# Second attention hop: the row mean taken directly behind the residual sums, with 40 filler matmuls instead of 48; mean layer: a tile's rows and turned rows in one transfer

## The chip, the cores and the metric

The kernel runs on one core of a Trainium2 chip. The metric is the time of one execution on the device, in microseconds (us), the median of three runs. A profile is one further execution, recorded by the hardware profiler. Engines are PE (TensorE), DVE (VectorE), ACT (ScalarE), POOL (GpSimd) and SP (SyncE), which issues most of the transfers here. "SPq", "DVEq" and so on are the sequencers of these engines: they load registers, compute with them, wait for semaphores, and hand work to the engine.

## What is computed

Four graph layers run over 50000 nodes of 256 values and 25000 edges, each followed by a residual sum and a layer norm. The two that the change touches are the first layer and the second hop of the third:

```python
# layer 0 (the kernel's mean layer)
agg = segment_sum(edge_weight[:, None] * x[dst], src)
out = concatenate([agg, x], axis=1) @ W.T
out = (out - mu) * rsqrt(var + 1e-5) * gamma + beta
x = layernorm(x + relu(out))
...
# layer 2 (attention), two hops
e = leaky(sum(([x[head], x[tail]] @ fc_w.T + fc_b) * rel_e, axis=-1))
w = exp(e - max of the head's edges) / their sum
x = sum over the head's edges of w * x[tail], plus x
x = x / max(norm(x), 1e-12)
...
x = layernorm(x_before_layer_2 + x)
```

## The kernel before

The kernel is a row of phases with a barrier between them: sorting the edges, the mean layer (`l0`), a message phase and relation layer twice, two attention hops (`l2a`, `l2b`), and the last layer. Rows lie in 391 tiles of 128 nodes. An *item* is a tile together with up to 128 of its edges. Every engine runs its own program over the items. There is no scheduler: the order on each engine is the hand-written tuple of steps, each with a number that says how many pairs (or octets) it runs ahead of the loop's count, and semaphores tie the engines together.

**Mean layer** (`mean_layer`, from L772). Items are done in pairs, a ring of 8 slots (`RING`), with a loop body of 4 pairs. `load_groups` gives the number of loop turns, items divided by 8 and rounded up. Per item PE sums the gathered edge rows into `ps_a` (L879) and multiplies the tile's turned rows (L889) and the sums (L892) by the weights; ACT takes `ps_b` and does squares and the last scaling (L767); DVE does the rest. SP (`move_tiles`, L145 on) issues per item three transfers of 128 KB: the rows `x` and the turned rows `x_t` into their slots (L160), and the result (L186). At the head of each loop turn it reads three lists of 8 row numbers into registers (L153). POOL (`gather_rows`) issues two indirect gathers per pair of items (L215), and between them (`between`) scatters for a later phase (L289), 200 of `item_records` and 20 of `rel_source_rows`, six for every five pairs. It waits for PE's sums of the pair four earlier before it reuses a slot.

**Second hop** (`attention_hop` with `last_hop`). Items are done in octets of 8, the loop body has two octets, and `load_hops` gives the number of turns, items divided by 16 and rounded up. In one octet's turn of the loop, with the lines that the prediction uses:

- DVE: `add_residual` of octet 0 (L1976, 8 sums over rows that also leave the row sum), `find_slots` (L1716, its sequencer reads 8 slot numbers into registers), `scores` (L1898 to L1905), `divide` (L1924 to L1929), `add_up` in two halves (L1914), with `centre` (L732, minus the row mean) between the halves, `add_self` (L1940), `maximum` (L1945 to L1957), `have_square` (L1964), `find_nodes` (L1885 on), and small steps of an inverse root up to L1631.
- ACT: `norm.square` of the octet (L741), which needs the mean; `measure` (L2018), `decay` (L2027, needs `minus` from L1957), guesses (L1614, L1616), `chances` (L2035), two copies to `hot` (L2043), and the last scaling (L767).
- PE: sums of 8 items (L2079), `spread` (L2089, L2091), 48 fillers (L700), `turn_chances` first half (L2098), 4 fillers, second half, `look_up` (L2111), 4 fillers. A filler is a matmul of zeros whose result nobody reads; `keep_busy` writes them.

A `pass_wait` is a wait of the sequencer by itself, followed by an increment; a plain `wait_ge` goes into the instruction behind it.

Of the kernel before, what the change touches and what calls it, by code (L numbers as in the profile page):

```python
# [30 lines left out]
P = 128  # L31
# [164 lines left out]
            sp.sem_inc(s["passed"], 1)  # L196


def gather_rows(pool, graph, s, index, gathered, source, extra=0, field=OTHER, count=N_NODES, between=None):
# [12 lines left out]
    fixed = TILES // RING  # L212

    def gather_by(slot, rows):
        pool.indirect_dma_start(gathered[:, slot, 0:D], None, source[0:count, :], bass.IndirectOffsetOnAxis(ap=rows, axis=0),  # L215
                                bounds_check=limit, oob_is_err=False).then_inc(s["in_g"][slot // 2], 16)

    def gather(pair, slot):
        both = slice(slot, slot + 2)
        pool.tensor_copy(index[:, both, 0], graph.meta[:, bass.ds(pair * 2, 2), field].bitcast(I32))\  # L220
            .then_inc(s["index_copied"], 1)
        pool.wait_ge(s["index_copied"], pair + 1)
        pool.sem_inc(s["passed"], 1)
        for k in (slot, slot + 1):
            gather_by(k, index[:, k, :])

    groups = load_groups(pool, graph)
    for pair in range(fixed * PAIRS):
        if pair >= PAIRS:
            pool.wait_ge(s[s["g_last"]], pair * 2 + 2 - RING)  # L230
        for item in (2 * pair, 2 * pair + 1):
            gather_by(item % RING, graph.meta[:, item, field:field + 1].bitcast(I32))
        if between is not None:
            between(pair)
    pool.sem_inc(s["index_copied"], fixed * PAIRS)
    with pool.Fori(fixed - 1, groups) as g:
        for n in range(PAIRS):
            pair = g * PAIRS + n
            pool.wait_ge(s[s["g_last"]], pair * 2 + 2)
            pool.sem_inc(s["passed"], 1)  # L240
            gather(pair + PAIRS, 2 * n)
    for n in range(extra // 2):
        pool.wait_ge(s[s["g_last"]], groups * RING + 2 * n + 2)
        pool.sem_inc(s["passed"], 1)
        gather((groups + 1) * PAIRS + n, 2 * n)
    for n in range(PAIRS):
        pool.wait_ge(s["in_g"][n], (groups + 1 + (2 * n < extra)) * 32)
        pool.sem_inc(s["passed"], 1)
# [445 lines left out]
        eng.wait_ge(sem, self.item + 2)  # L694


def keep_busy(pe, c, spare, n):

    for _ in range(n):
        pe.matmul(spare, c.ones_b[:], c.zero_row[:], start=True, stop=True)  # L700


def run_pairs(eng, graph, steps):


    groups = load_groups(eng, graph)
    for n in range(-max(ahead for _, ahead in steps), 0):
        for step, ahead in steps:
            if n + ahead >= 0:
                step(Pair(0, n + ahead))  # L710
    with eng.Fori(0, groups) as g:
        for n in range(PAIRS):
            for step, ahead in steps:
                step(Pair(g, n + ahead))


class Norm:
# [51 lines left out]
                .then_inc(s["out_ready"] if done is None else done, 1)  # L769


def mean_layer(nc, c, graph, w, gamma, beta, eps, x_in, x_in_t, x_out, relations, edges, records, rel_source):  # L772

    with Phase(nc, "l0") as ph:
        x, gathered, agg_t, x_t, products, scaled, shifted, summed, result = (
            ph.sb(k, [P, RING, D], F32) for k in ("x", "gathered", "agg_t", "x_t", "products", "scaled", "shifted",
                                                  "summed", "result"))
# [7 lines left out]
        s["in_xt"] = [ph.sem(f"in_xt{k}") for k in range(RING)]  # L785
        s_records, s_sources = ([ph.pool_dma_sem(f"{n}{k}") for k in range(2)] for n in ("records", "sources"))
        inner, outer = Norm(ph, "inner", eps), Norm(ph, "outer", eps)
        with nc.Block() as block:
            @block.sync
            def _(sp):  # L790
                later = ((x_t, x_in_t, s["in_xt"], s["b_done"], 6),)
                move_tiles(sp, graph, s, x, x_in, result, x_out, later, lead=2)

            @block.gpsimd
            def _(pool):
                by_dst = Scatter(pool, s_records, records[:], edges.place, lambda column: edges.records[:, column, :])
                sources = Scatter(pool, s_sources, rel_source[:], relations.place,
                                  lambda column: relations.source[:, column:column + 1])
# [8 lines left out]
                gather_rows(pool, graph, s, index, gathered, x_in, extra=2, between=between)  # L807
                by_dst.finish()
                sources.finish()
                assert by_dst.sent == EC and sources.sent == EC - SOURCES_BEFORE  # L810

            @block.vector
            def _(dve):
# [18 lines left out]
                def combine(pair):  # L832
# [8 lines left out]
                    for j, k in pair.each():  # L841
                        pass_wait(dve, s, s["in_x"][k], (pair.lap + 1) * 16)
                        dve.wait_ge(s["shifted"], j + 1)
                        dve.scalar_tensor_tensor(summed[:, k, :], shifted[:, k, :], 0.0, x[:, k, :], ALU.max, ALU.add,
                                                 accum_out=outer.sum[:, k:k + 1]).then_inc(s["summed"], 1)

                def centre_outer(pair):
# [7 lines left out]
                make(Pair(0, 0))  # L855
                run_pairs(dve, graph, ((lambda p: inner.invert(dve, p), 1), (centre_inner, 2), (combine, 1),
                                       (lambda p: outer.invert(dve, p), 0), (lambda p: outer.shift(dve, p), 0),
                                       (accumulate, 5), (centre_outer, 1)))

# [1 line left out]
            def _(act):  # L861
                def take(pair):
                    for j, k in pair.each():
# [4 lines left out]
                run_pairs(act, graph, ((lambda p: outer.spread(act, p, summed), 0),  # L868
                                       (lambda p: inner.spread(act, p, products), 2), (take, 3),
                                       (lambda p: outer.apply(act, s, p, result, summed), 0)))  # L870

# [1 line left out]
            def _(pe):  # L873
# [7 lines left out]
                        last.then_inc(s["a_done"], 1)  # L881

                def product(pair):
                    for j, k in pair.each():
                        if not isinstance(j, int) or j >= 4:
                            pe.wait_ge(s["products"], j - 3)
                        pe.wait_ge(s["in_xt"][k], (pair.lap + 1) * 16)
                        for i in range(2):
                            pe.matmul(ps_b[k % 4], x_t[:, k, i * P:(i + 1) * P], w[:, 2 + i, :], start=(i == 0), stop=False)  # L889
# [796 lines left out]
def attention_hop(nc, c, graph, name, node_rows, w, x_in, x_out, residual=None):  # L1686
# [6 lines left out]
    with Phase(nc, name) as ph:  # L1693
# [46 lines left out]
        with nc.Block() as block:  # L1740
# [133 lines left out]
            def _(dve):  # L1874
# [195 lines left out]
            def _(pe):  # L2070
# [172 lines left out]
def build(nc, a, out):  # L2243
# [3 lines left out]
    with ExitStack() as ctx:  # L2247
# [13 lines left out]
        with ExitStack() as first:  # L2261
# [7 lines left out]
            with ExitStack() as prep:  # L2269
                def sb_prep(name, shape, dt):  # L2270
                    return prep.enter_context(nc.sbuf_tensor(name, shape, dt))
                for g, n in zip(graphs, ("src", "dst")):
# [5 lines left out]
            mean_layer(nc, c, by_src, w.l0, w.gamma, w.beta, w.eps, a["x"], a["x_turned"], x1, relations, edges,  # L2278
                       item_records[1], rel_source)
            count_edges_and_message(nc, c, graphs, node_rows, relations, item_records[1], rel_source, "ma", a["L1_gnn_W1"], x1,  # L2280
                                    messages)
# [9 lines left out]
def laid_out(inputs):  # L2291
# [2 lines left out]
    x = np.zeros((ALL_ROWS, D), np.float32)  # L2294
    x[:N_NODES] = a["x"]
    a["x"] = x
    a["x_turned"] = x.reshape(-1, P, 2, P).transpose(0, 3, 2, 1).reshape(ALL_ROWS, D)
# [22 lines left out]
```

## Time and profile before

| | us |
|---|---|
| median of 3 runs | 6965.96 (6964.8 to 6974.53) |
| profiled execution | 6984.61 |
| its span, first to last instruction | 6982.7 |
| mean granted clock of PE over the span | 0.933 |

Of the span, PE is busy 90%, DVE 76%, ACT 61%, POOL 56%. The mean layer lies at 702 to 1677 us and the second hop at 4926 to 5914 us. A clock of 1.00 is 2.4 GHz, 0.50 is 1.2 GHz. Matmuls are pipelined: the duration that is shown for one reaches past the start of the next, so what one costs is read from start to start.

### The profile page before, as it was taken

What the parts mean: (1) busy time and instruction counts of PE and PEld (TensorE: products, weight loads), DVE (VectorE), ACT (ScalarE), POOL (GpSimd) and SP (SyncE); (2) the same over time, 40 slices, a digit from 0 to 9 for tenths busy, and PEclk for the clock granted to TensorE, in tenths of its full rate; (3) what the DMA queues carried; (4) which work ended last, traced back from release to release, by engine and by line L of the source; (5) the groups of instructions that cost most, each with busy time, mean ns of one, the idle gap of its engine ahead of it and who ended that gap; (6) DMA issues with size and microseconds to landing.
All of it is one profiled execution on the core that took longest, in us unless ns stands there. A gap on an engine that the chain in (4) does not pass through costs nothing. (4 is left out here: it accounts for less than half of the span.)

```text
span 6982.7 us, 169103 instructions
## 1 busy us (share of the span) xinstructions
PE 6298.9 (90%) x37102; PEld 5098.3 (73%) x37103; DVE 5285.4 (76%) x18168; ACT 4280.0 (61%) x14748; POOL 3904.1 (56%) x3592
## 2 busy tenths in 40 slices
PE   5676899997789998989999899999899998999999
PEld 2222788886688887769999788888566666888887
DVE  9887888887655654247777677777688887899998
ACT  0000899995214443238888677777588787677777
POOL 6677777775736666754444444444444444444443
PEclk9555999998879999999999899999899999999999
DMA  1200666666656666667777666665577676444443
GB/s 40 6 2 8 182 193 193 194 194 192 182 154 192 199 197 186 198 186 222 222 222 222 178 185 187 186 187 173 176 221 216 205 221 184 123 126 127 128 127 118
DMA packets 1224976, 1161.36 MB, mean 166 GB/s; under 512 B 314483, under 2 KB 1152523, under 8 KB 1224094
## 3 DMA queue, kind: packets, MB, share of 16 engines
q1 hardware_dynamic: 1067230, 943.02, 43.9%
q0 software_dynamic: 157632, 217.06, 13.3%
q8 instruction: 42, 0.69, 0.0%
q14 instruction: 72, 0.59, 0.0%
HBM read 946.93 MB, written 395.69 MB: 192 GB/s over the span
## 5 line engine op out<-in xcount | busy, mean ns | idle before, releaser
L215 POOL DMA_INDIRECT l_gathered<-x,by_dst_meta x384 | 433.6, 1129 | 547.7 <-PE l_ps_a L1571 485.8
L1836 POOL DMA_INDIRECT l2b_gathered<-z,by_src_meta x408 | 431.1, 1057 | 534.9 <-PE l2b_ps_g L2079 419.6
L1836 POOL DMA_INDIRECT l2a_gathered<-x,by_src_meta x408 | 431.1, 1057 | 453.8 <-PE l2a_ps_g L2079 338.1
L215 POOL DMA_INDIRECT l1b_gathered<-messages,by_dst_meta x384 | 395.3, 1029 | 437.8 <-PE l1b_ps_b L1434 376.8
L215 POOL DMA_INDIRECT l1a_gathered<-messages,by_dst_meta x384 | 432.1, 1125 | 206.7 <-PE l1a_ps_b L1434 141.7
L700 PE MATMUL l2b_ps_x<-zero_row,ones_b 128*128 128x392 bf16 x2912 | 510.1, 330 | 0.0
L215 POOL DMA_INDIRECT l_gathered<-in_x,by_src_meta x384 | 417.7, 1088 | 130.7 <-issue 113.9
L889 PE MATMUL l_ps_b<-l_w,l_x_t 128*128 128x256 f32 x1592 | 416.2, 384 | 38.8 <-DMA l_x_t<-in_x_turned 37.8
L865 ACT ACT_TABLE_LOAD x1 | 1.3, 1283 | 702.6 <-PEq L129 702.6
L1432 PE MATMUL l1b_ps_b<-root,l1b_x_t 128*128 128x256 f32 x1600 | 425.8, 389 | 0.0
L1432 PE MATMUL l1a_ps_b<-root,l1a_x_t 128*128 128x256 f32 x1584 | 415.6, 385 | 3.8 <-DVE l1a_hot L670 1.6
L700 PEld LDWEIGHTS l2b_ps_x<-zero_row,ones_b 128*128 128x128 bf16 x2912 | 286.1, 100 | 178.8 <-issue 0.9
L1388 ACT ACTIVATE l1a_x_t<-l1a_ps_x,by_dst_first 128x256 f32<-128x256 f32 x400 | 167.6, 470 | 401.4 <-PE l1a_ps_x L1420 401.4
L892 PE MATMUL l_ps_b<-l_w,l_agg_t 128*128 128x256 f32 x1592 | 409.0, 379 | 0.0
L1590 PE MATMUL l_ps_b<-l_w,l_mix_t 128*128 128x256 f32 x1592 | 396.5, 392 | 8.9 <-DVE l_mix_t L1506 8.8
L1338 DVE SCALAR_TENSOR_TENSOR l1a_total<-l1a_total,by_dst_keep,l1a_ps_b 128x256 f32<-128x256 f32 x394 | 187.1, 475 | 270.3 <-PE l1a_ps_b L1434 270.3
L1586 PE MATMUL l_ps_b<-l_w,l_x_t 128*128 128x256 f32 x1592 | 384.3, 384 | 1.0 <-ACT l_x_t L1551 1.0
L633 PE MATMUL sort_ps_rank<-sort_onehot,not_before 125*125 125x392 bf16 x400 | 234.6, 587 | 162.6 <-DVE sort_junk L583 162.6
L1590 PEld LDWEIGHTS l_ps_b<-l_w,l_mix_t 128*128 128x128 f32 x1592 | 286.3, 189 | 114.7 <-DVE l_mix_t L1506 83.6
L633 PEld LDWEIGHTS sort_ps_rank<-sort_onehot,not_before 125*125 125x125 bf16 x400 | 72.0, 180 | 384.8 <-DVE sort_junk L583 384.8
L889 PEld LDWEIGHTS l_ps_b<-l_w,l_x_t 128*128 128x128 f32 x1592 | 284.5, 191 | 86.7 <-DMA l_x_t<-in_x_turned 31.2
L892 PEld LDWEIGHTS l_ps_b<-l_w,l_agg_t 128*128 128x128 f32 x1592 | 303.0, 190 | 41.4
(402 smaller groups left out, 20682.5 us busy)
## 6 DMA issues: line engine op xcount, KB each, us to landing
x<-l1b_result SPq DMA_DIRECT2D x400, 152.0 KB, 3.0
z<-l2a_result SPq DMA_DIRECT2D x400, 152.0 KB
l2a_x<-x SPq DMA_DIRECT2D x53, 1024.0 KB
l2b_x<-z SPq DMA_DIRECT2D x53, 1024.0 KB
l1b_x<-h SPq DMA_DIRECT2D x408, 128.0 KB
l1b_res<-x SPq DMA_DIRECT2D x408, 128.0 KB
l2b_res<-x SPq DMA_DIRECT2D x51, 1024.0 KB
l_x_t<-in_x_turned SPq DMA_DIRECT2D x406, 128.0 KB
```

Of the source, the lines that this page charges most:

```text
L215: pool.indirect_dma_start(gathered[:, slot, 0:D], None, source[0:count, :], bass.IndirectOffsetOnAxis(ap=rows, axis=0), bounds_check=limit ...
L633: pe.matmul(rank[o][0:EP, :], c.not_before[0:EP, 0:EP], onehot[0:EP, o, k, :], start=False, stop=True, skip_group_check=True)
L700: pe.matmul(spare, c.ones_b[:], c.zero_row[:], start=True, stop=True)
L865: act.activation(products[:, k, :], ps_b[k % 4], ACT.Identity, accum_out=inner.sum[:, k:k + 1])\
L889: pe.matmul(ps_b[k % 4], x_t[:, k, i * P:(i + 1) * P], w[:, 2 + i, :], start=(i == 0), stop=False)
L892: last = pe.matmul(ps_b[k % 4], agg_t[:, k, i * P:(i + 1) * P], w[:, i, :], start=False, stop=(i == 1))
L1338: dve.scalar_tensor_tensor(total[:, k, :], total[:, (k - 1) % RING, :], graph.keep[:, bass.ds(j, 1)], ps_b[k // 2 % 2][:, k % 2, :], ALU.m ...
L1388: act.activation(x_t[:, k, :], ps_x[k // 2 % 2][:, k % 2, :], ACT.Copy, scale=graph.first[:, bass.ds(j, 1)]).then_inc(s["xt"], 1)
L1432: pe.matmul(sums, x_t[:, k, f * P:(f + 1) * P], root[:, f, :], start=(f == 0), stop=False)
L1586: pe.matmul(ps_b[k % 4], x_t[:, k, i * P:(i + 1) * P], w1[:, i, :], start=(i == 0), stop=False)
L1590: last = pe.matmul(ps_b[k % 4], mix_t[:, k, i * P:(i + 1) * P], w2[:, i, :], start=False, stop=(i == 1))
L1836: pool.indirect_dma_start(gathered[:, k, :], None, x_in[0:N_NODES, :], bass.IndirectOffsetOnAxis(ap=rows, axis=0), bounds_check=limit, oob ...
```

## The change

Three edits. In the second hop, `centre` moves on DVE from between the halves of `add_up` to directly behind `add_residual`, ahead of `find_slots`. The row of 48 fillers there becomes 40. In the mean layer, the host lays rows and turned rows side by side (`x_both`, 512 values a row), and one transfer of 256 KB brings both, into a ring of 16 slots; the loop body has 8 pairs, so the number of items is rounded up to a multiple of 16 and no longer of 8. The gathers still read `x`.

```diff
+        both = ph.sb("both", [P, HOP, 2 * D], F32)
+        x, x_t = both[:, :, 0:D], both[:, :, D:2 * D]
...
-                later = ((x_t, x_in_t, s["in_xt"], s["b_done"], 6),)
-                move_tiles(sp, graph, s, x, x_in, result, x_out, later, lead=2)
...
+                def load(row, slot):
+                    sp.dma_start(both[:, slot, :], x_both[bass.ds(row, P), :]).then_inc(in_both[slot], 16)
+
+                for half in range(2):
+                    rows = rows_of(load_regs, LOAD, half * RING)
+                    for k in range(RING):
+                        load(rows[k], half * RING + k)
...
+                hops = load_hops(sp, graph)
+                with sp.Fori(0, hops) as g:
+                    for half in range(2):
+                        first = g * HOP + half * RING
+                        rows = rows_of(store_regs, STORE, first)
+                        next_rows = rows_of(load_regs, LOAD, first + HOP)
+                        for k in range(RING):
+                            sp.wait_ge(s["summed"], first + (k + 1))
+                            load(next_rows[k], half * RING + k)
+                            sp.wait_ge(s["out_ready"], first + (k + 1))
+                            sp.dma_start(x_out[bass.ds(rows[k], P), :], result[:, k, :]).then_inc(s["stored"][k], 16)
...
-    groups = load_groups(pool, graph)
+    groups = load_hops(pool, graph) * 2 if wide else load_groups(pool, graph)
...
-                run_pairs(pe, graph, ((product, 3), (gather_sum, 5)))
+                run_wide_pairs(pe, graph, ((product, 3), (gather_sum, 5)))
...
-                    steps = [(add_residual, 0), (find_slots, 1), (scores, 2), (divide, 1), (part(add_up, 0), 1), (centre, 0), (part(add_up, 1), 1),
+                    steps = [(add_residual, 0), (centre, 0), (find_slots, 1), (scores, 2), (divide, 1), (part(add_up, 0), 1), (part(add_up, 1), 1),
...
-                        (spread, 2), (part(fill, 48), 2), (part(turn_chances, 0), 2), (part(fill, 4), 2),
+                        (spread, 2), (part(fill, 40), 2), (part(turn_chances, 0), 2), (part(fill, 4), 2),
```

The move on DVE, second hop, in the loop body's second octet. Before, from the last residual sum to behind the mean:

```order
L1976 SCALAR_TENSOR_TENSOR l2b_y,l2b_norm_sum<-l2b_y,l2b_inv_root,l2b_res 128x256
L1716 ISA
L1716 TENSOR_LOAD by_src_table
L1657 REGISTER_ALU
L1898 TENSOR_TENSOR l2b_both<-l2b_ps_s,l2b_gathered 128x192
...
L1914 SCALAR_TENSOR_TENSOR l2b_agg<-l2b_agg,l2b_shrink,l2b_ps_g 128x256 x2
L732 TENSOR_SCALAR l2b_norm_minus_mean<-l2b_norm_sum 128x8
```

and of the changed kernel, in the same place:

```order
L2035 SCALAR_TENSOR_TENSOR l2b_y,l2b_norm_sum<-l2b_y,l2b_inv_root,l2b_res 128x256
L758 TENSOR_SCALAR l2b_norm_minus_mean<-l2b_norm_sum 128x8
L1775 ISA
L1775 TENSOR_LOAD by_src_table
L1716 REGISTER_ALU
L1957 TENSOR_TENSOR l2b_both<-l2b_ps_s,l2b_gathered 128x192
```

The mean, which waits for the last residual sum, now stands ahead of the sequencer's read of the slot numbers (TENSOR_LOAD), and with it ahead of `scores`. Line numbers grow by 26 or 59.

On SP, mean layer, the head of the loop body up to the third transfer. Before:

```order
L153 TENSOR_LOAD by_src_table
L154 ISA
L153 ISA
L153 TENSOR_LOAD by_src_table
L154 ISA
L153 ISA
L153 TENSOR_LOAD by_src_table
L154 ISA
L160 DMA l_x<-in_x 128x256
L160 DMA l_x_t<-in_x_turned 128x256
L186 DMA x<-l_result 128x256
```

and of the changed kernel:

```order
L821 TENSOR_LOAD by_src_table
L822 ISA
L821 ISA
L821 TENSOR_LOAD by_src_table
L822 ISA
L825 DMA l_both<-in_x_both 128x512
L845 DMA x<-l_result 128x256
```

Eight items cost SP three lists and 24 transfers before, and two lists and 16 transfers now.

## Rows read from the trace of the kernel before

**Rows 1.** Stretches: busy us of PE, PEld, DVE, ACT, POOL; clock, DMA share, GB/s
```profile
900.00:1200.00 300.00, 284.67 (x1524) 247.53 (x1523) 262.43 (x1080) 274.79 (x1016) 237.65 (x205) 1.00 0.68 193
5100.00:5400.00 300.00, 289.03 (x1801) 207.40 (x1799) 262.01 (x911) 252.25 (x990) 130.86 (x126) 1.00 0.73 218
```
**Rows 2.** Timeline of SP, mean layer: start us, us, engine, line, operation, names
```profile
1250.12 0.36 SPq L186 DMA_DIRECT2D x<-l_result  x1
1255.97 0.34 SPq L160 DMA_DIRECT2D l_x<-in_x  x1
...
1268.99 0.36 SPq L186 DMA_DIRECT2D x<-l_result  x1
```
**Rows 3.** What POOL waited for, 900 to 1200 us: total, times, longest
```profile
POOL l_gathered L215 <- issue: 38.5, 126, 0.3
POOL item_records L289 <- issue: 23.6, 77, 0.3
```
**Rows 4.** Timeline of POOL, mean layer: its first gather, and one of the last
```profile
705.63 1.05 POOL L215 DMA_INDIRECT l_gathered<-in_x,by_src_meta  x1 [1.65 <-issue]
...
1567.38 1.02 POOL L215 DMA_INDIRECT l_gathered<-in_x,by_src_meta  x1 [0.30 <-issue]
```
**Rows 5.** Timeline of PE, mean layer: first sums, and two pairs at the end
```profile
710.19 2.08 PE L879 MATMUL l_ps_a<-l_hot,l_gathered 128*128 128x128 f32 x8 [11.49 <-DMA l_gathered<-in_x,by_src_meta]
...
1653.27 1.05 PE L879 MATMUL l_ps_a<-l_hot,l_gathered 128*128 128x128 f32 x8
...
1657.62 1.05 PE L879 MATMUL l_ps_a<-l_hot,l_gathered 128*128 128x128 f32 x8
```
**Rows 6.** Timeline of SP: mean layer's last store, next phase's first transfer
```profile
1669.92 0.36 SPq L186 DMA_DIRECT2D x<-l_result  x1
1676.98 0.33 SPq L949 DMA_DIRECT2D rel_index<-rel_source_rows  x1
```
**Rows 7.** Timeline of DVE, second hop: loop body's first octet, sums and scores
```profile
5219.28 0.49 DVE L1976 SCALAR_TENSOR_TENSOR l2b_y<-l2b_y,l2b_inv_root,l2b_res 128x256 f32<-128x256 f32 x1 [1.04 <-DMA l2b_res<-x]
...
5222.54 0.35 DVE L1898 TENSOR_TENSOR l2b_both<-l2b_ps_s,l2b_gathered 128x192 f32<-128x192 f32 x1
...
5223.71 0.17 DVE L1905 SCALAR_TENSOR_TENSOR l2b_score<-l2b_plain 128x8 f32<-128x8 f32 x1
```
**Rows 8.** Timeline of DVE, second octet of the same loop body
```profile
5237.62 0.49 DVE L1976 SCALAR_TENSOR_TENSOR l2b_y<-l2b_y,l2b_inv_root,l2b_res 128x256 f32<-128x256 f32 x1 [0.42 <-DVE l2b_inv_root L1631]
...
5241.23 0.36 DVE L1898 TENSOR_TENSOR l2b_both<-l2b_ps_s,l2b_gathered 128x192 f32<-128x192 f32 x1 [0.27 <-PE l2b_ps_s L2111]
```
**Rows 9.** DVE's sequencer at L1716 and L664, 5219.5 to 5224.5
```profile
L1716 DVEq TENSOR_LOAD <-by_src_table x1: 594/594/594, 5220.6 to 5220.6; - x1
...
L664 DVEq ALU_OP  x2: 40/40/40, 5223.7 to 5223.9; - x2
```
**Rows 10.** Timeline of PE, second hop: fillers, and `turn_chances` in both octets
```profile
5190.35 8.12 PE L700 MATMUL l2b_ps_x<-zero_row,ones_b 128*128 128x392 bf16 x48
5199.25 0.66 PE L2098 MATMUL l2b_ps_e<-ident,l2b_chance 128*128 128x128 f32 x4 [0.77 <-ACT l2b_chance L2035]
...
5217.83 0.66 PE L2098 MATMUL l2b_ps_e<-ident,l2b_chance 128*128 128x128 f32 x4 [0.28 <-ACT l2b_chance L2035]
```
**Rows 11.** Timeline of PE: the two longest of these waits, and the third
```profile
5123.58 0.66 PE L2098 MATMUL l2b_ps_e<-ident,l2b_chance 128*128 128x128 f32 x4 [1.29 <-ACT l2b_chance L2035]
...
5428.41 0.66 PE L2098 MATMUL l2b_ps_e<-ident,l2b_chance 128*128 128x128 f32 x4 [1.98 <-ACT l2b_chance L2035]
...
5546.95 0.66 PE L2098 MATMUL l2b_ps_e<-ident,l2b_chance 128*128 128x128 f32 x4 [1.74 <-ACT l2b_chance L2035]
```
**Rows 12.** Stretch behind the second, PE: busy us (x), clock, DMA share, GB/s
```profile
5429.00:5439.00 10.00, 10.00 (x38) 0.51 0.41 109
```
**Rows 13.** Timeline of DVE: first sum of this octet, and of the next
```profile
5428.94 0.48 DVE L1976 SCALAR_TENSOR_TENSOR l2b_y<-l2b_y,l2b_inv_root,l2b_res 128x256 f32<-128x256 f32 x1 [0.42 <-DVE l2b_inv_root L1631]
...
5452.43 0.48 DVE L1976 SCALAR_TENSOR_TENSOR l2b_y<-l2b_y,l2b_inv_root,l2b_res 128x256 f32<-128x256 f32 x1 [1.04 <-issue]
```

More of the change, by code:

```diff
@@ L196, in move_tiles, with gather_rows @@
             sp.sem_inc(s["passed"], 1)
-def gather_rows(pool, graph, s, index, gathered, source, extra=0, field=OTHER, count=N_NODES, between=None):
+def gather_rows(pool, graph, s, index, gathered, source, extra=0, field=OTHER, count=N_NODES, between=None, wide=False):
     limit = pool.alloc_register(f"limit_{s['name']}")
@@ L694, in wait_items, with __init__, each_wide @@
         eng.wait_ge(sem, self.item + 2)
+class WidePair(Pair):
+    def __init__(self, group, n):
+        super().__init__(group * 2, n)
+        self.wide = 2 * n % HOP
+        self.wide_lap = group + n // RING
+    def each_wide(self):
+        return [(self.item + q, self.slot + q, self.wide + q) for q in range(2)]
 def keep_busy(pe, c, spare, n):
@@ L714, in run_pairs, with run_wide_pairs @@
                 step(Pair(g, n + ahead))
+def run_wide_pairs(eng, graph, steps):
+    hops = load_hops(eng, graph)
+    for n in range(-max(ahead for _, ahead in steps), 0):
+        for step, ahead in steps:
+            if n + ahead >= 0:
+                step(WidePair(0, n + ahead))
+    with eng.Fori(0, hops) as g:
+        for n in range(RING):
+            for step, ahead in steps:
+                step(WidePair(g, n + ahead))
 class Norm:
@@ L769, in apply, with mean_layer @@
                 .then_inc(s["out_ready"] if done is None else done, 1)
[L772 removed]
+def mean_layer(nc, c, graph, w, gamma, beta, eps, x_in, x_both, x_out, relations, edges, records, rel_source):
     with Phase(nc, "l0") as ph:
[L775 to L777 removed]
+        gathered, agg_t, products, scaled, shifted, summed, result = (
+            ph.sb(k, [P, RING, D], F32) for k in ("gathered", "agg_t", "products", "scaled", "shifted", "summed", "result"))
+        both = ph.sb("both", [P, HOP, 2 * D], F32)
+        x, x_t = both[:, :, 0:D], both[:, :, D:2 * D]
         index = ph.sb("index", [P, RING, 1], I32)
@@ L784, in mean_layer @@
             s[k] = ph.sem(k)
-        s["in_xt"] = [ph.sem(f"in_xt{k}") for k in range(RING)]
+        in_both = s["in_x"] + [ph.sem(f"in_x{k}") for k in range(RING, HOP)]
         s_records, s_sources = ([ph.pool_dma_sem(f"{n}{k}") for k in range(2)] for n in ("records", "sources"))
@@ L790, in _, with rows_of @@
             def _(sp):
-                later = ((x_t, x_in_t, s["in_xt"], s["b_done"], 6),)
-                move_tiles(sp, graph, s, x, x_in, result, x_out, later, lead=2)
+                store_regs, load_regs = ([sp.alloc_register(f"l0_{n}_{k}") for k in range(RING)] for n in ("store", "load"))
+                def rows_of(regs, field, first_item):
+                    sp.load(regs, graph.table[0:1, field, bass.ds(first_item, RING)])
+                    return [sp.snap(r, min_val=0, max_val=ALL_ROWS - P) for r in regs]
+                def load(row, slot):
[4 more added lines that the diff above has]
+                        load(rows[k], half * RING + k)
+                sp.wait_ge(s["zeroed"], 2)
+                for slot in range(RING):
+                    sp.dma_start(x_out[ROWS + slot * P:ROWS + (slot + 1) * P, :], result[:, slot, :])\
+                        .then_inc(s["stored"][slot], 16)
+                hops = load_hops(sp, graph)
[9 more added lines that the diff above has]
+                            sp.dma_start(x_out[bass.ds(rows[k], P), :], result[:, k, :]).then_inc(s["stored"][k], 16)
+                for slot in range(RING):
+                    sp.wait_ge(s["stored"][slot], (hops * 2 + 1) * 16)
+                    sp.sem_inc(s["passed"], 1)
+                for slot in range(HOP):
+                    sp.wait_ge(in_both[slot], (hops + 1) * 16)
+                    sp.sem_inc(s["passed"], 1)
             @block.gpsimd
@@ L805, in between @@
                             sources.send(SOURCES_BEFORE + n - EC)
-                gather_rows(pool, graph, s, index, gathered, x_in, extra=2, between=between)
+                gather_rows(pool, graph, s, index, gathered, x_in, extra=2, between=between, wide=True)
                 by_dst.finish()
@@ L840, in combine @@
                                                  ALU.mult, ALU.add).then_inc(s["shifted"], 1)
-                    for j, k in pair.each():
-                        pass_wait(dve, s, s["in_x"][k], (pair.lap + 1) * 16)
+                    for j, k, m in pair.each_wide():
+                        pass_wait(dve, s, in_both[m], (pair.wide_lap + 1) * 16)
                         dve.wait_ge(s["shifted"], j + 1)
-                        dve.scalar_tensor_tensor(summed[:, k, :], shifted[:, k, :], 0.0, x[:, k, :], ALU.max, ALU.add,
+                        dve.scalar_tensor_tensor(summed[:, k, :], shifted[:, k, :], 0.0, x[:, m, :], ALU.max, ALU.add,
                                                  accum_out=outer.sum[:, k:k + 1]).then_inc(s["summed"], 1)
@@ L854, in _ @@
                 dve.sem_inc(s["acc"], 1)
-                make(Pair(0, 0))
-                run_pairs(dve, graph, ((lambda p: inner.invert(dve, p), 1), (centre_inner, 2), (combine, 1),
+                make(WidePair(0, 0))
+                run_wide_pairs(dve, graph, ((lambda p: inner.invert(dve, p), 1), (centre_inner, 2), (combine, 1),
                                        (lambda p: outer.invert(dve, p), 0), (lambda p: outer.shift(dve, p), 0),
@@ L883, in product @@
                 def product(pair):
-                    for j, k in pair.each():
+                    for j, k, m in pair.each_wide():
                         if not isinstance(j, int) or j >= 4:
                             pe.wait_ge(s["products"], j - 3)
-                        pe.wait_ge(s["in_xt"][k], (pair.lap + 1) * 16)
+                        pe.wait_ge(in_both[m], (pair.wide_lap + 1) * 16)
                         for i in range(2):
-                            pe.matmul(ps_b[k % 4], x_t[:, k, i * P:(i + 1) * P], w[:, 2 + i, :], start=(i == 0), stop=False)
+                            pe.matmul(ps_b[k % 4], x_t[:, m, i * P:(i + 1) * P], w[:, 2 + i, :], start=(i == 0), stop=False)
                         pe.wait_ge(s["acc"], j + 2)
```

6 lines of the change are left out of this document (3 added, 3 removed).

## The prediction

> **What bounds the kernel now.** First the stretches of both places. In the mean layer POOL's busy time [rows 1] and its gaps, none above 0.3 us [rows 3], make 237.65 + 38.5 + 23.6 = 299.75 of 300 us: POOL is at its pace. SP is too. From the last store of one loop turn to that of the next is 18.87 us for 8 items, and between that store and the next transfer lie 5.85 us [rows 2], in which it reads three lists of row numbers. So (18.87 - 5.85) / 23 = 0.57 us is one transfer's pace. Both engines do 8 items in about 19 us: POOL's 183 pairs from 705.63 to 1567.38 [rows 4] are 4.71 us each, 18.8 us per 8 items. PE could go faster: at the end, with its gathers ahead of it, two pairs lie 1657.62 - 1653.27 = 4.35 us apart [rows 5].
>
> In the second hop PE is busy 289 of 300 us [rows 1], but the loop is not PE's: much of that are fillers, 48 in a row with 8.12 / 49 = 0.166 us from one to the next, the last being shown twice as long [rows 10]. Behind them PE waits 0.77 us in the turn that ends the first octet and 0.28 us in the other, for ACT's `chances`. DVE waits almost nowhere: its first sum follows its own inverse root (0.42 us) or the 1.04 us of the loop's head [rows 7, 8]. The loop goes by DVE's steps, and by the ring DVE, `decay` on ACT, `chances`, PE. From the wait at 5123.58 to that at 5428.41 lie 16 octets [rows 11]: 304.83 / 16 = 19.05 us each, 38.1 us a turn. The first octet's 5237.62 - 5219.28 = 18.34 us [rows 7, 8] leave 19.8 us for the second, with the loop's head. 25 turns make the hop.
>
> **Mean layer, part by part.** *Transfers.* 8 items now cost SP 16 transfers and two lists instead of 24 and three: 16 x 0.57 + 5.85 x 2/3 = 13.0 us. That is below POOL's 18.8, so SP stops being a bound. POOL's work is unchanged, and it stays the next one, so the middle of the layer gains nothing. What ends is SP's lag at the tail. *Two halves of 8 pairs.* The count is rounded up to 16 items: 392 becomes 400, which is 4 pairs more. POOL's gather at 1567.38 is that of pair 184 of 200 [rows 4], and all scatters are issued by then. Its sums can follow by 710.19 - 705.63 = 4.6 us [rows 4, 5], at 1572. From there on PE is the bound with 20 more pair steps at 4.35 us: 1572 + 87 = 1659. I put the last store about 3 us behind, at 1662, and the next phase's first transfer 1676.98 - 1669.92 = 7.06 us behind that [rows 6], at 1669: **-8 us**. From below, if SP's lag was also what held the pairs before (11 us of PE's lag behind POOL at the end), -13. From above, if POOL's gathers or the rows' larger transfers make PE later by three pairs' time, +6.
>
> **Second hop: the mean.** The edit moves one 128x8 instruction, which itself costs 0.11 us where it stood and 0.12 where it goes. What matters is what it stands ahead of. DVE's sequencer reads the slot numbers in 0.594 us at 5220.6, in the midst of the eight sums, which it has handed over by then: the read is hidden, and `scores` start at 5222.54, 3.26 us behind the first sum [rows 7, 9]. The sums wait for nothing that runs on DVE just then. The mean waits for the last of them. What a waiting instruction does to the sequencer the trace shows at L1905, which waits for the step before it: it starts at 5223.71, and the two register steps of L664 that stand behind it start at 5223.7 and 5223.9 [rows 7, 9], although nothing else held them. So the sequencer stood until L1905 went, and I take it that it will stand at the mean too. Then the order is mean at +3.36, 0.12 for it to go, 0.60 for the read, 0.40 for some ten register steps of 40 ns each, `scores` at **+4.48**. Net in the first octet 4.48 - 3.26 = 1.22, less the 0.11 saved later: 1.11 us. In the second octet `scores` start at 3.61 [rows 8], of which 0.27 is a wait for PE that is covered now; the median over the octets is 3.51, so 4.48 - 3.51 - 0.11 = 0.86. Together 2.0 us a turn, 25 turns: 50 us. Waits for the residual rows ahead of the first sum, some 4 us over the hop, vanish in it: **+46 us**. From below: if the read is still hidden, the term is 2 x -0.11 x 25 = -5. From above, if the read takes its place among busy transfers and is slower by half, +60. I take 46, since L1905 and L664 are the same sequencer in the same loop.
>
> The Trainium skill says otherwise. By "Perfetto Trace Analysis", section "DVE / Act Engine Instruction", a DVE instruction is pushed into a wait queue, and the sequencer decodes the next one before its semaphores are satisfied. By that rule the read stays hidden and the sum loses its 46 us; rows 9 show L664 behind L1905's start, which speaks against it.
>
> **Second hop: 40 fillers.** They aren't on the ring's path, so the 8 that go save nothing by themselves; PE waits 8 x 0.166 = 1.33 us longer. To that comes what `chances` are later by: the waits become 0.77 + 1.11 + 1.33 = 3.2 us and 0.28 + 0.86 + 1.33 = 2.5 us. Nobody needs PE earlier; what the fillers keep up is its clock. Of the waits at this place, 1.29 us left the clock at 1.00, and the two longest, 1.74 and 1.98 us [rows 11], were followed by a clock of 0.51, which is the lower of the two levels, 1.2 GHz [rows 12]. The octet in which it ran low, a second one of its turn, took 5452.43 - 5428.94 = 23.49 us from first sum to first sum [rows 13], where its place takes 19.8, or 19.6 without the waits for residual rows that are in the 46 already: 3.9 us more. The other one took 22.61 (5547.50 to 5570.11), 3.0 more. Both new waits are longer than those that were followed by a fall. But while the matmuls run low, PE is late and has no wait at all, so the next wait comes an octet later: I count one fall per turn. It costs (3.9 + 3.0) / 2 = 3.5, less the 0.9 us by which `scores` now come later in any case, so that a late PE holds them less: 2.6 us. 25 x 2.6 = 65, less the 7 us of the two falls that are in the time already: **+58 us**. From below, none: -7. From above, each at 3.9: 98 - 7 = 91.
>
> **Sum.** -8 + 46 + 58 = +96 us. The profiled execution took 6984.61 us, 6982.7 of it the span; with the sum it is 7080.6. It lies 18.65 us above the median of the runs, which I carry over: **7062 us**. Its own range, with the ends above where they go together: 7025 to 7100.
>
> **Rivals.**
> *The read is exposed, but the clock mostly stays.* For it: only two waits above 1.7 us are there to judge by, and the one of 1.29 us left no mark on the clock [rows 11]. Against it: both were followed by a fall. -8 + 46 - 7 = +31: 6997 us.
> *The read stays hidden, and the clock falls.* The scores come where they did, and the waits are 0.77 - 0.11 + 1.33 = 2.0 and 1.5 us: the first is as long as those that fell. Half of 25 turns at 3.5 is 44, less 7; with -8 and -5: +24, 6990 us. If every turn falls, 7033.
> *Nothing is exposed (the other side).* The read stays hidden as before, by a sequencer that goes on past the mean, and waits of 2.0 us leave the clock mostly up. Then the mean saves 0.11 us in each of 50 octets, 5 us, and the tail of the mean layer 8: 6953 us, not slower. It decides at one point: whether `scores` begin within 0.4 us of the last sum's end or a full 1.1 us behind.
> *The joined transfer doesn't do what it says.* If the rows' transfer, twice as large, keeps 8 items at 19 us on SP, the 8 more items cost 19 us instead of -8: 27 us on top of any case. Rows 2 speak against it: SP's pace goes by the number of its transfers.
>
> **How the numbers follow.** The forecast has 0.55, exposed with the clock up 0.15, hidden with falls 0.12, nothing exposed 0.13, and 0.05 are left for the last rival and what I don't see. The range must reach from the forecast's top, 7100, down past the second and third case: from 6970 it leaves out the fourth, and little above. A measurement of this kernel tells 0.2%, 14 us, from no change: the fourth case lies on that bound, at -13, so its 0.13 goes half to faster and half to same. With some of the third and of the rest: faster 0.10, same 0.12, slower 0.78.
>
> **What would show it.** In the profile of the changed kernel: in the second hop `scores` 4.5 us behind the octet's first sum, with the read of the slot numbers just behind the mean; PE's waits ahead of `turn_chances` at 2.5 us and more in octets whose matmuls ran at full clock; rows of stretches at 0.50 in about every turn, and turns of some 43 us instead of 38.2. In the mean layer SP waits, POOL doesn't, and the next phase begins at about 1669. The forecast is wrong if `scores` follow the last sum as closely as before, or if the clock stays at 1.00 through waits of 2.5 us. It is too low if both octets of a turn fall.

## The result, and the profile after

The changed kernel takes 7044.17 us (median of 4, 7038.37 to 7052.11), the kernel before 6970.24 us beside it (median of 4, 6964.8 to 6975.01). The ratio is 1.0107, with a 95% interval of 1.009 to 1.0125: 74 us slower. 7062 was forecast, in a range of 6970 to 7100. One of all the executions below, one of `centre`, ran slow as a whole (9934 us, at a granted clock of 0.60) and stays out of every ratio.

The profiled execution took 7040.41 us, its span 7038.7, against the 6982.7 of the span before: 56.0 us more. From the first instruction of each phase to that of the next, in us:

| | before | after |
|---|---|---|
| mean layer, from the end of the sort | 996.3 | 992.4 |
| first message phase | 407.1 | 395.3 |
| first relation layer | 681.3 | 686.5 |
| second hop, to its last instruction | 1015.2 | 1078.4 |
| last layer | 1066.6 | 1069.8 |

The other phases differ by less than 1 us. The hop makes 63 us, the mean layer -4. The two phases behind the mean layer are untouched by the change and differ by -12 and +5 all the same. In the message phase PE's granted clock goes up and down, and it was 0.84 in the one execution and 0.86 in the other (1677 to 2076 us); in the relation layer it is 0.98 in both, and the +5 there and the +3 of the last layer stay unexplained.

In the second hop, DVE's timeline of the changed kernel, a first octet of the loop body (start us, duration us, engine, line, operation; answers to [rows 7]):

```profile
5185.61 0.48 DVE L2035 SCALAR_TENSOR_TENSOR l2b_y<-l2b_y,l2b_inv_root,l2b_res 128x256 f32<-128x256 f32 x1 [1.04 <-issue]
...
5188.46 0.48 DVE L2035 SCALAR_TENSOR_TENSOR l2b_y<-l2b_y,l2b_inv_root,l2b_res 128x256 f32<-128x256 f32 x1
5188.98 0.17 DVE L758 TENSOR_SCALAR l2b_norm_minus_mean<-l2b_norm_sum 128x8 f32<-128x8 f32 x1
5190.12 0.36 DVE L1957 TENSOR_TENSOR l2b_both<-l2b_ps_s,l2b_gathered 128x192 f32<-128x192 f32 x1 [0.96 <-PE l2b_ps_s L2170]
```

and its sequencer's read of the slot numbers in the same octet (answers to [rows 9]):

```profile
L1775 DVEq TENSOR_LOAD <-by_src_table x1: 596/596/596, 5189.1 to 5189.1; - x1
```

The mean goes at 3.37 us behind the first sum, the read starts 0.1 us behind the mean, and `scores` follow at 5190.12 - 5185.61 = 4.51 us, with DVE idle for 0.96 us ahead of them. Before, the read lay in the midst of the sums and `scores` were at 3.26. The profile names PE as what ended these 0.96 us, since PE's semaphore is the last that `scores` looked at. PE's look-up for them:

```profile
5187.52 2.14 PE L2170 MATMUL l2b_ps_s<-l2b_head,l2b_hot_t 128*128 x16
```

It ends at 5189.66, 0.46 us before `scores` start; in the median of the first octets it ends 1.6 us before. What DVE stood for then is the register read and the steps behind it, which have no semaphore. Over the 25 first octets `scores` are at 4.52 us in the median, over the second ones at 4.70, where 3.26 and 3.51 stood before. The second ones are of two kinds. In the seven without a fall of the clock `scores` start at 4.43, with PE done 0.8 us and more earlier: that is the read. In the other 18 the clock had fallen (below), and they start at 4.54 to 5.74, at once behind PE's look-up, which is late there.

What PE waits for ahead of `turn_chances` (answers to [rows 10, 11]): one of the short waits, and two that were followed by a low clock, for 10 us and for 3 us,

```profile
5101.58 0.66 PE L2157 MATMUL l2b_ps_e<-ident,l2b_chance 128*128 128x128 f32 x4 [1.60 <-ACT l2b_chance L2094]
...
5122.49 0.66 PE L2157 MATMUL l2b_ps_e<-ident,l2b_chance 128*128 128x128 f32 x4 [3.74 <-ACT l2b_chance L2094]
...
5204.77 0.79 PE L2157 MATMUL l2b_ps_e<-ident,l2b_chance 128*128 128x128 f32 x4 [2.14 <-ACT l2b_chance L2094]
```

and PE alone in the stretches around two of them (us, busy us and instructions, granted clock, transfers' share, GB/s; answers to [rows 12]):

```profile
5117.00:5122.00 5.00, 1.75 (x11) 1.00 0.93 292
5123.20:5133.40 10.20, 10.20 (x38) 0.50 0.33 91
5199.00:5202.00 3.00, 3.00 (x20) 1.00 0.97 299
5205.20:5208.40 3.20, 3.20 (x16) 0.50 0.69 227
```

The fall at 5123.2 lasts 10.2 us, that at 5205.2 ends after 3.4 us. The length of the wait alone does not decide whether one follows. Of the 22 waits of 2.5 us and more at this place, the longest 4.04 us, seven were not followed by a fall, such as this one (the row of PE's wait, and PE in the stretch behind it):

```profile
5370.58 0.66 PE L2157 MATMUL l2b_ps_e<-ident,l2b_chance 128*128 128x128 f32 x4 [2.97 <-ACT l2b_chance L2094]
```
```profile
5370.60:5389.00 18.40, 16.87 (x106) 1.00 0.67 190
```

Of seven waits of 2.12 to 2.15 us, six were followed by one. In the changed kernel there are 6 of the long kind and 14 of the short within the octets, where before there were two, of 7 and 10 us. The mean clock over the hop was 0.99 and is 0.94:

```profile
4940.00:5920.00 980.00, 859.69 (x5092) 0.94 0.67 201
```

So the hop's 49 distances from one octet's first sum to the next sort themselves:

| octets | before | after |
|---|---|---|
| first of the turn | 25 of 18.38 us | 25 of 19.56 |
| second, clock up | 22 of 19.70 | 7 of 19.76 |
| second, short fall | - | 11 of 20.99 |
| second, fall of 7 to 10 us | 22.61, 23.49 | 6 of 23.55 |
| sum | 938.9 | 999.5 |

25 x (19.56 - 18.38) = 29.5 us by the read, 24 x (19.76 - 19.70) = 1.4 us in the second octets, and by the clock 11 x 1.23 + 6 x 3.79 - (2.91 + 3.79) = 29.6 us. That is all of the 60.6. It is a reading of one execution of each kernel; no run on this chip takes the parts of the change one by one.

In the mean layer SP now waits for results (total us, times, longest, 900 to 1200 us; it never did before). The next two fences are PE's sums near the end ([rows 5]) and SP's last store ([rows 6]):

```profile
SPq L845 <- ACT l_result L793: 122.0, 51, 4.7
```
```profile
1571.61 1.05 PE L938 MATMUL l_ps_a<-l_hot,l_gathered 128*128 128x128 f32 x8
...
1662.89 1.05 PE L938 MATMUL l_ps_a<-l_hot,l_gathered 128*128 128x128 f32 x8
```
```profile
1666.23 0.34 SPq L845 DMA_DIRECT2D x<-l_result  x1
1673.72 0.33 SPq L1008 DMA_DIRECT2D rel_index<-rel_source_rows  x1
```

The last store lies 3.3 us behind the last sums, where SP lagged by 10 us and more before ([rows 6]).

### The profile page after: what moved, and what is told of

It is laid out like the page before. It is cut to its first block and busy times, and to the rows that moved or that the text cites. A ratio compares the mean times of both kernels' runs of the same rounds, so it can differ in the third digit from the quotient of the medians.

```text
span 7038.7 us, 166416 instructions
## 1 busy us (share of the span) xinstructions
PE 6276.0 (89%) x36782; PEld 5101.8 (72%) x36783; DVE 5310.0 (75%) x18236; ACT 4304.8 (61%) x14812; POOL 3926.2 (56%) x3604
## 5 line engine op out<-in xcount | busy, mean ns | idle before, releaser
L712 PE MATMUL l2b_ps_x<-zero_row,ones_b 128*128 128x392 bf16 x2496 | 456.9, 337 | 0.0
L948 PE MATMUL l_ps_b<-l_w,l_both 128*128 128x256 f32 x1624 | 421.6, 382 | 0.0
L1645 PE MATMUL l_ps_b<-l_w,l_x_t 128*128 128x256 f32 x1592 | 384.2, 384 | 1.0 <-ACT l_x_t L1610 1.0
L712 PEld LDWEIGHTS l2b_ps_x<-zero_row,ones_b 128*128 128x128 bf16 x2496 | 250.0, 102 | 156.3 <-issue 9.0
L948 PEld LDWEIGHTS l_ps_b<-l_w,l_both 128*128 128x128 f32 x1624 | 296.1, 192 | 32.4
```

Of the source, the lines that this page charges most:

```text
L948: pe.matmul(ps_b[k % 4], x_t[:, m, i * P:(i + 1) * P], w[:, 2 + i, :], start=(i == 0), stop=False)
L1645: pe.matmul(ps_b[k % 4], x_t[:, k, i * P:(i + 1) * P], w1[:, i, :], start=(i == 0), stop=False)
```

## The experiments

All experiments ran on three other chips, and each of these is slower: the kernel before takes 7814 us on the chip of `centre`, `fill40`, `mean` and `behind`, 7978 on that of `small_free`, `small_waits`, `fill56` and `after_again`, and 7821 on that of the runs whose names end in `_2`. Each kernel is compared with the kernel before on its own chip, as a ratio with its 95% interval, and the us beside it are by that ratio. The first part below is what that difference is, since nearly every time hangs on it.

**Where the slower chips lose time.** Not everywhere: the sort and the last layer take about what they took (681 and 1068 us). The old mean layer takes 1200 to 1235 us instead of 996, the first hop 1322 to 1406 instead of 943, the second, in its old order, 1131 to 1183 instead of 1015. The message phases and the first relation layer lose less, the second message phase 50 us and more on its 297. The untouched first hop differs by up to 57 us between the profiled executions on two of these chips (1322 to 1379). In the mean layer, the steps on SP's sequencer at the store's line, 1000 to 1300 us, of the kernel before on the chip of the forecast (count: shortest/median/longest in ns):

```profile
L186 SPq FUSED_REGOPS  x125: 37/37/37, 1000.1 to 1298.7; - x125
L186 SPq MOVE x<-l_result x125: 29/29/29, 1000.1 to 1298.8; - x125
```

and of the same code in `fill40_2` on a slower chip:

```profile
L186 SPq FUSED_REGOPS  x102: 4/37/702, 1000.2 to 1297.3; - x102
L186 SPq MOVE x<-l_result x102: 3/29/706, 1000.3 to 1297.3; - x102
```

A step between registers, 29 ns in each of 125 cases, now takes up to 706 ns, and the profile shows no wait at it. The second hop's fillers on PE show the same. The idle time ahead of them that no semaphore ended (us, times), in the kernel before on the chip of the forecast:

```profile
  issue: 0.9, 5
```

in the changed kernel on that chip:

```profile
  issue: 9.0, 51
```

and on the slower chips, in `mean_2` with 48 fillers, and in `fill56_2` with 56:

```profile
  issue: 299.4, 514
```
```profile
  issue: 352.5, 689
```

So engines there stand between instructions that depend on nothing, PE 0.5 to 0.6 us at a time in the mean (299.4 / 514, 352.5 / 689). That the instructions themselves come late would explain it; that was not tested by itself and stays open. What follows for reading the runs: on these chips SP's many small steps bound the old mean layer, and in the second hop DVE isn't the only bound. DVE's own distances, such as that of `scores`, stay as exact as on the chip of the forecast in octets without such a stall.

**The mean alone moved** (`centre`, and again as `centre_2`).

```diff
-steps = [(add_residual, 0), (find_slots, 1), (scores, 2), (divide, 1), (part(add_up, 0), 1), (centre, 0), (part(add_up, 1), 1),
+steps = [(add_residual, 0), (centre, 0), (find_slots, 1), (scores, 2), (divide, 1), (part(add_up, 0), 1), (part(add_up, 1), 1),
```

> The kernel before with one edit: the mean directly behind the residual sums, ahead of the slot numbers' read; 48 fillers and the old mean layer stay. Theory (the read is exposed behind the waiting mean): scores 4.4 to 4.5 us behind the first sum in every octet, first octets 19.5 us instead of 18.34, second ones about 19.7; PE's waits ahead of turn_chances 1.7 and 1.4 us, so a few clock falls at most; +30 to +45 us against before. Rival (the missing fillers are the cause, the mean is harmless): scores at 3.3 to 3.5 us, 0 to -5 us.

> The kernel before with the mean ahead of the read, 48 fillers, once more. On a chip of 6970 us: scores at 4.5 us, first octets 19.5, second ones 19.7 us; waits of 1.7 us and less, few falls: +30 to +45 us. On a slower chip: +40 us or so, with the same 4.5 us.

Measured: 1.0055 (1.0031 to 1.008) and 1.0058 (1.0037 to 1.0079) of the kernel before, 43 and 45 us. `scores` at 4.52 and 4.51 us in the first octets and 4.43 in the second, on both chips. Undisturbed first octets take 19.5 us. The move alone costs time, with all 48 fillers in place, and the rival that holds it harmless is out. The few falls of the clock that I expected were 31 and 28, against 21 and 20 in the old hop on the same chips (`mean`, `mean_2`, below), so a part of the 43 and 45 us is the clock's.

**40 fillers alone** (`fill40`, and again as `fill40_2`).

```diff
-(spread, 2), (part(fill, 48), 2), (part(turn_chances, 0), 2),
+(spread, 2), (part(fill, 40), 2), (part(turn_chances, 0), 2),
```

> The kernel before with one edit: 40 fillers instead of 48. Theory (fewer fillers only let the clock fall, and only where a wait becomes long): scores stay at 3.3 and 3.5 us, first octets stay at 18.34 us, PE's waits become 2.1 and 1.6 us, and between none and 25 clock falls follow the 2.1 us ones: 0 to +30 us. Rival (the fillers alone make the 74 us): +60 us or more.

> The kernel before with 40 fillers, once more. On a chip of 6970 us: scores at 3.3 and 3.5 us, first octets 18.34 us, PE's waits 2.1 and 1.6 us; about half of the 25 turns with a clock fall, most of them short ones of 1.2 us: +5 to +25 us. Rival (the fillers are the bulk of the loss): +50 us or more. On a slower chip: within 0.5% either way.

Measured: 1.005 (1.0031 to 1.0069) and 1.0022 (1.0004 to 1.0041), 39 and 17 us. `scores` stay at 3.25 us in the first octets. PE's clock over the hop, in `fill40_2` and, for comparison on the same chip, in `mean_2`, which has the old hop:

```profile
5710.00:6750.00 1040.00, 893.13 (x4974) 0.90 0.62 184
```
```profile
5560.00:6590.00 1030.00, 907.31 (x5409) 0.96 0.64 188
```

The missing fillers cost something too, by the rows through the clock, and more than I expected in the first of the two. The two agree within their intervals.

**The mean layer alone** (`mean`, and again as `mean_2`): the changed kernel with the old order on DVE and 48 fillers.

> The changed mean layer alone, the second hop as before. Theory: SP waits, POOL sets the pace, the next phase begins 2 to 5 us earlier than before by its own start, hop as before: -4 us, no measurable difference. Rival (the layer's 8 more items or larger transfers are a part of the loss): +10 us or more.

> The changed mean layer alone, once more. If this chip runs the kernel before in about 6970 us: next phase 2 to 5 us earlier, -4 us, no measurable difference. If it takes 7800 us or more for it, as the chips of the runs so far: the mean layer 150 us or more shorter.

Measured: 0.9835 (0.9817 to 0.9853) and 0.9819 (0.9775 to 0.9863), 129 and 142 us faster (135 and 134 by the medians). The layer takes 1041 and 1042 us, where the old one takes 1204.8 and 1208.3 on the chip of `mean` and 1199.6 and 1201.3 on that of `mean_2`. For `mean` I had expected no difference; on the chip of the forecast that still stands by its trace, -4 us. On these chips it is the largest effect of all. What PE waited for in the old layer, 1000 to 1300 us, `fill40_2`:

```profile
PE l_ps_b L889 <- DMA l_x_t<-in_x_turned: 51.1, 24, 5.4
```

PE stood for the turned rows, that is for SP, which never waited, not for a free slot either; so it is SP's work that held the layer, and not the shorter ring. With two transfers per item instead of three, SP has time to wait itself even there (`mean_2`):

```profile
SPq L845 <- ACT l_result L793: 5.5, 6, 1.5
SPq L825 <- DVE l_summed L903: 1.7, 3, 0.7
```

**The mean behind the read** (`behind`): the changed kernel with one exchange of places.

```diff
-steps = [(add_residual, 0), (centre, 0), (find_slots, 1), (scores, 2),
+steps = [(add_residual, 0), (find_slots, 1), (centre, 0), (scores, 2),
```

> The changed kernel with the mean one step later: behind the read of the slot numbers, ahead of scores. The same instruction with the same wait. Theory (what costs is that the sequencer stands at the mean ahead of the read): read hidden again, scores at 3.4 to 3.6 us, first octets about 18.5 us, falls as in the kernel with 40 fillers alone; 40 us or more faster than the changed kernel. Rival (the cost is the mean's wait on DVE itself, or ACT's squares coming early): scores late or periods long as in the changed kernel, within 10 us of it.

Measured: 0.9866 (0.9843 to 0.9889). The same instruction with the same wait, and `scores` at 3.78 us:

```profile
6201.80 0.17 DVE L758 TENSOR_SCALAR l2b_norm_minus_mean<-l2b_norm_sum 128x8 f32<-128x8 f32 x1
6202.20 0.36 DVE L1957 TENSOR_TENSOR l2b_both<-l2b_ps_s,l2b_gathered 128x192 f32<-128x192 f32 x1 [0.24 <-issue]
```
```profile
L1775 DVEq TENSOR_LOAD <-by_src_table x1: 598/598/598, 6199.7 to 6199.7; - x1
```

The read is back in the midst of the sums (6198.42 is the first of them). Of the 4.52 - 3.26 = 1.26 us, 4.52 - 3.78 = 0.74 were the read, and 0.52 are the mean with what is left behind its wait; I had expected 3.4 to 3.6, a little too little. The changed kernel wasn't run on this chip, so the 40 us by which this was to be faster stay open. Against `mean` on the same chip it is 29 us slower: 40 fillers and the half microsecond.

**A small instruction without and with the wait** (`small_free`, `small_waits`): the kernel before, and between the sums and the read a 128x8 instruction of the mean's form whose result is not used. The line with `wait_items` is in `small_waits` alone.

```diff
+def small_step(o):
+    o.wait_items(dve, s["summed"])
+    dve.tensor_scalar(spare_8[:], graph.keep[:, 0:OCT], -1.0 / D, None, ALU.mult)
...
-steps = [(add_residual, 0), (find_slots, 1), (scores, 2),
+steps = [(add_residual, 0), (small_step, 0), (find_slots, 1), (scores, 2),
```

> The kernel before, with one more small instruction on DVE in the second hop between the residual sums and the slot numbers' read: 128x8, of the mean's form, over values that were ready long ago, result unused, and without a wait. Theory (only a waiting instruction holds the sequencer): the read stays hidden, scores at 3.3 to 3.4 us, octets 0.1 us longer, +0 to +6 us. Rival (any instruction between the sums and the read exposes it, by its place alone): scores at 4.4 us or more, +30 us.

> The same small instruction in the same place, now with the mean's wait for the last residual sum; the mean itself stays between the halves of add_up. Theory: scores at 4.5 us as in the changed kernel, first octets 19.5 us; +30 to +50 us. Rival (it is the mean's result being early, ACT's squares starting before others, that costs): scores at 3.4 us, +0 to +6 us.

Without the wait, an undisturbed octet:

```profile
6870.21 0.49 DVE L1976 SCALAR_TENSOR_TENSOR l2b_y<-l2b_y,l2b_inv_root,l2b_res 128x256 f32<-128x256 f32 x1 [1.03 <-issue]
...
6873.47 0.16 DVE L1996 TENSOR_SCALAR l2b_spare<-by_src_keep 128x8 f32<-128x8 f32 x1
6873.55 0.35 DVE L1898 TENSOR_TENSOR l2b_both<-l2b_ps_s,l2b_gathered 128x192 f32<-128x192 f32 x1
```
```profile
L1716 DVEq TENSOR_LOAD <-by_src_table x1: 592/592/592, 6871.7 to 6871.7; - x1
```

With it, the first sum at 6340.77:

```profile
6344.14 0.17 DVE L1997 TENSOR_SCALAR l2b_spare<-by_src_keep 128x8 f32<-128x8 f32 x1
6345.28 0.36 DVE L1898 TENSOR_TENSOR l2b_both<-l2b_ps_s,l2b_gathered 128x192 f32<-128x192 f32 x1 [0.96 <-PE l2b_ps_s L2117]
```
```profile
L1716 DVEq TENSOR_LOAD <-by_src_table x1: 594/594/594, 6344.2 to 6344.2; - x1
```

3.34 against 4.51 us, by the wait alone: the place, the operation and its size are the same. Over all first octets the medians are 3.46 and 4.53 us. That settles why `scores` come late, and that the mean's result comes early has no part in it. In time: 0.9999 (0.9981 to 1.0016) and 1.0021 (1.0004 to 1.0038). The second is 17 us, less than the 30 to 50 expected: on this chip the octets average 22.8 us, and I take it that part of what DVE loses lies beside other stalls.

**More fillers** (`fill56`, and again as `fill56_2`; `after_again` is the changed kernel beside it).

```diff
-(spread, 2), (part(fill, 40), 2), (part(turn_chances, 0), 2),
+(spread, 2), (part(fill, 56), 2), (part(turn_chances, 0), 2),
```

> The changed kernel with 56 fillers instead of 40: 16 x 0.166 = 2.7 us more of them per octet. Theory (scores later make some +31 us, clock falls some +32 us of the second hop's 63): PE's waits ahead of turn_chances fall to 0.3 to 1.3 us, no clock falls, first octets 19.5, second ones 19.7 us; 25 to 35 us faster than the changed kernel. Rival (the fillers sit on the path once there are more): slower than the changed kernel, or equal, with octets above 20 us.

> The changed kernel with 56 fillers, once more. On a chip of 6970 us: no clock falls in the second hop, octets 19.5 and 19.7 us, +25 to +35 us against before, which is 40 us less than the changed kernel. On a slower chip: as the changed kernel there, 2% faster than before, since what the clock gives is spent on more instructions.

> The changed kernel again, beside the others on their chip. Scores at 4.5 us whatever the chip. If this chip runs the kernel before in about 6970 us: +74 us again. If it is one on which the kernel before takes about 7814 us: the mean layer gives back some 150 us there, so 7730 us.

Measured: `fill56` 0.9794 (0.9765 to 0.9823), `after_again` 0.9775 (0.9727 to 0.9822), `fill56_2` 0.989 (0.9851 to 0.9929). Here the changed kernel is 2.2% *faster* than the one before, since the mean layer gives 176 us (1058.0 against 1234); I had expected the kernel 84 us faster for it, on a chip of 7814 us, and it is 180. The clock went up with the fillers, in `after_again` and in `fill56`:

```profile
5585.00:6700.00 1115.00, 926.87 (x4995) 0.87 0.59 175
```
```profile
5570.00:6700.00 1130.00, 995.40 (x5804) 0.94 0.59 173
```

but the falls did not vanish as expected, 43 of 3.4 us are left, and the hop took 1219 and 1230 us: no gain. `fill56_2` was to be 2% faster and is 1.1%. 16 more instructions in each octet stand in the stalls shown above, and second octets go to 24.6 us. Whether 56 fillers would give back the 30 us on the chip of the forecast isn't answered by this; no run came to such a chip again.

**A kernel better than both** is `mean`: 1.7% and 1.8% faster than the kernel before on two slower chips, on one of them 70 us faster than `fill56_2`. On the chip of the forecast it wasn't run; by the trace there its mean layer would give 4 us.

## Why the prediction was right, and where it was off

*The read of the slot numbers behind the waiting mean.* Forecast: mean at +3.36, `scores` at +4.48; measured 3.37 and 4.51. The first octets' 1.11 us was 1.18 in the time of the octet. The step that failed is the second octet's 0.86 us, which was 0.06. `scores` came later there by as much as I said (4.43 where the clock stayed up), but that octet had other waits of DVE in it, for which the same work now comes just in time: DVE's idle time is 2.1 us in such an octet before and 2.0 after. In the kernel before, the second octet that begins at 5199.77 had 0.18 us ahead of `scores`, and

```profile
5205.80 2.03 DVE L1914 SCALAR_TENSOR_TENSOR l2b_agg<-l2b_agg,l2b_shrink,l2b_ps_g 128x256 f32<-128x256 f32 x4 [0.43 <-PE l2b_ps_g L2079]
```

then 0.24 at L1885, and the waits for residual rows; I had taken off the first and the last. Of all 46 us there were 31.

With the wait the read starts 0.1 us behind the small instruction's start, without it 1.8 us ahead of it: the sequencer does not go on past an instruction that waits. By the Trainium skill, "Perfetto Trace Analysis", section "DVE / Act Engine Instruction", it would; here the measurement decides against that.

*The clock.* One fall per turn was forecast, 25; there were 20, 17 of them where they lengthen an octet. Their price was the mis-sized term: 3.5 us, less 0.9, from the two falls that the trace before had, both long. Two thirds of the new ones end after 3.4 us and cost 1.23 us; the long ones cost 3.79, and nothing is to be taken off. 29.6 us against 58. Where 3.2 and 2.5 us stood in the forecast, PE's waits were 2.7 to 4.0 (2.1 in three) and 1.3 to 2.4 us, in the median 1.6. The forecast named a clock that stays at 1.00 through waits of 2.5 us as a sign of being wrong. That sign is there in part: seven of 22 such waits left the clock up. So the rule behind the term, that a wait longer than the two of the trace before is followed by a fall, does not hold, and that the count came out near 25 is in part luck.

*The mean layer.* SP waits, POOL is at its pace, as forecast. -3.9 us instead of -8: the sums of the pair that I put at 1572 began at 1571.61, but 21 pairs followed and not 20 (1571.61 + 21 x 4.35 = 1663.0, and the last is at 1662.89). The layer began 0.9 us later as well.

*From profile to median.* The trace's sum was 40 us too high (96 against 56), and the forecast still only 18 us above the result. The 18.65 us by which the profiled execution lay above the median were carried over; the one of the changed kernel lies 3.8 us below its median. Some 12 us of the difference may be the first message phase, whose clock was lower in the profiled execution of the kernel before (0.84 against 0.86). A profile is one draw of such phases. Two errors partly cancelled, and that the time came out within 18 us is luck to that extent.

*The rivals.* That the read stays hidden is refuted, and with it the case on the other side. That the clock mostly stays up is half true: it fell 20 times in 25 turns, but for 3.4 us in 14 of them. That the joined transfer doesn't pay was wrong everywhere, and far more so than I could see: its worth depends on the chip.

## What to carry to other kernels

An instruction that must wait for the one ahead of it should not stand ahead of a register read or other steps of the sequencer: put the read first, where it hides behind queued work. A move that makes a critical engine later also lengthens the waits of the engine whose clock is being kept up, so it pays twice, and removing fillers in the same edit adds to that. A saturated queue of small transfers is worth relieving even where the trace shows another engine at the same pace: elsewhere it may be the bound by a wide margin.

## What the runs showed of the hardware

The same program differs by 12 to 14.5% between chips (6970 us against 7814 to 7978), in some phases by nearly half and in others not at all, and the difference shows as stalls between instructions without any wait, of up to 0.7 us on SP's sequencer (`fill40_2`) and of 0.5 to 0.6 us in the mean on PE (`mean_2`, `fill56_2`). The sign of this change goes with it: 1.0107 on one chip, 0.9775 on another. In the octets of the changed kernel a lowered clock lasted 3.4 us in 14 cases and 10.2 us in 6. Waits of 2.14 us were followed by the low level, those of 1.6 us there were not, and of eight waits of 2.97 us two were and six were not. On DVE, steps of the sequencer start right behind the start of an instruction that waits (0.1 us, `after`, `small_waits`), and 1.8 us ahead of one that does not (`small_free`).
